# The carried row of a running prefix sum: an accumulating transfer sent by POOL in place of a plain transfer and a one-row addition on DVE

## The reference, cut to what matters

```
Tv = cheb(k)[:, :, :, j] * v                       # j = 0 .. 5 terms
kv_prefix = cumsum(Tv, over the 1024 positions)    # per batch row
ks_prefix = cumsum(cheb(k).sum(-1), over positions)
out = sum_j(Tq * beta * kv_prefix) / (sum_j(sum(Tq) * beta * ks_prefix) + 1e-7)
x = x + (out @ W_out.T) * silu(layernorm(moe(xn) + xn))
```

## Time and profile before

| | us |
|---|---|
| median of 3 runs | 885.68 |
| lowest, highest | 882.62, 885.87 |
| the profiled execution's own time | 883.1 |
| its span | 881.3 |
| DVE busy | 652.7 (74%), 1667 instructions |
| PE busy | 583.4 (66%) |
| ACT busy | 444.7 (50%) |
| POOL busy | 434.3 (49%) |

### The profile page before, as it was taken

How to read it: one execution, slowest core, us unless ns; L and a number is a source line. 1 busy time by engine, 2 the same in 40 slices (tenths; PEclk the granted TensorE clock), 3 DMA queues, 4 the chain that set the end, 5 groups by cost and what they waited for, 6 DMA issues and landing times.

```text
span 881.3 us, 21985 instructions
## 1 busy us (share of the span) xinstructions
PE 583.4 (66%) x7047; PEld 394.8 (45%) x7047; DVE 652.7 (74%) x1667; ACT 444.7 (50%) x1075; POOL 434.3 (49%) x697
## 2 busy tenths in 40 slices
PE   1888788878788878853544277777777777732120
PEld 0465555555555555542222145555555555421110
DVE  4588777777777777755878078989898989737766
ACT  1365555545555555521343277878787878400001
POOL 3134444544444555442777444444444444277873
PEclk9999999999999999985575599999999999955555
DMA  9920000000000000000111303333333332112221
GB/s 236 344 59 3 3 3 0 0 0 0 0 0 0 0 0 0 2 1 12 52 49 66 99 25 97 97 97 97 97 97 97 97 97 97 36 48 66 57 66 51
DMA packets 64527, 49.53 MB, mean 56 GB/s; under 512 B 10057, under 2 KB 55377, under 8 KB 64465
## 3 DMA queue, kind: packets, MB, share of 16 engines
q1 hardware_dynamic: 59328, 39.74, 14.4%
q0 software_dynamic: 5136, 9.02, 3.8%
HBM read 18.83 MB, written 18.35 MB: 42 GB/s over the span
## 4 chain that ended last, share of the span: by engine, by line
PE 32%; DVE 24%; POOL 17%; issue 17%; ACT 5%; DMA 2%; DVEq 2%; SPq 0%; POOLq 0%; ACTq 0%
POOL experts_sb L541 7%; POOL xbuf L528 7%; PE m_ps L988 4%; PE p_ps L869 4%; PE e_ps L1000 4%; DVE yts L1306 3%; PE q_ps L899 2%; PE y_ps L951 2%; ACT vd L603 2%; PE p_ps L944 2%; DVE x_all L1151 2%; DVE pr L1303 2%; DVE rot L1120 2%; ACT xs L608 1%; PE y_ps L832 1%
## 5 line engine op out<-in xcount | busy, mean ns | idle before, releaser
L576 ACT ACTIVATE pexp<-e_ps 128x512 f32<-128x512 f32 x128 | 76.4, 597 | 76.3 <-PE e_ps L816 74.7
L988 PE MATMUL m_ps<-xs,wb 128*128 128x512 f16 x276 | 80.6, 404 | 19.7 <-issue 18.4
L1087 DVE TENSOR_REDUCE mneg<-m_ps 128x4 bf16<-128x512 f32 x128 | 84.5, 681 | 5.1 <-PE m_ps L783 5.0
L541 POOL DMA_INDIRECT experts_sb<-ybuf,slots x64 | 66.1, 1033 | 28.7 <-issue 18.5
L528 POOL DMA_INDIRECT xbuf<-x,slots x64 | 63.3, 990 | 33.9 <-issue 19.2
L492 POOL COPY xs<-xs 128x128 f16<-128x128 f16 x32 | 12.8, 400 | 107.3 <-ACT xs L608 107.3
L603 ACT COPY vd<-p_ps 64x64 f32<-64x64 f32 x128 | 27.0, 211 | 73.1 <-DVE early L1122 70.8
L1046 PE MATMUL e_ps<-b_sb,cwt 8*128 8x128 f32 x64 | 16.6, 436 | 63.7 <-ACT cwt L744 63.7
L832 PE MATMUL y_ps<-pexp,vd 128*32 128x128 f32 x512 | 55.1, 284 | 2.7 <-ACT pexp L576 0.6
L1262 DVE TENSOR_SCALAR early<-p_ps 128x256 f32<-128x256 f32 x32 | 13.6, 424 | 55.3 <-ACT vs L650 55.3
L960 PE MATMUL p_ps<-eye_sb,yn 128*128 128x128 f32 x32 | 11.6, 364 | 63.7 <-DVE yn L1311 63.7
(11 more groups left out here) (218 smaller groups left out, 2125.6 us busy)
## 6 DMA issues: line engine op xcount, KB each, us to landing
wb<-experts_sb SPq DMA_DIRECT2D x46, 256.0 KB, 2.4
xbuf<-zero_sb SPq DMA_DIRECT2D x23, 256.0 KB, 4.3
xs<-xbuf SPq DMA_DIRECT2D x23, 256.0 KB, 3.0
ybuf<-rt SPq DMA_DIRECT2D x23, 256.0 KB, 2.5
experts_sb<-in_experts_w SPq DMA_DIRECT2D x8, 512.0 KB, 6.5
x_all<-in_x SPq DMA_DIRECT2D x8, 256.0 KB, 5.5
xbuf<-x,slots POOLq DMA_INDIRECT x64, 2.2
experts_sb<-ybuf,slots POOLq DMA_INDIRECT x64, 2.6
```

Of the source, the lines that this page charges most:

```text
L541: nc.gpsimd.indirect_dma_start(yg[:, 2 * (B * n + b) + k, :], None, ybuf, bass.IndirectOffsetOnAxis(ap=slots[:, k, B * n + b:B * n + b + 1 ...
L576: nc.scalar.activation(pexp[:, j, :, :], e_ps[j % 2][:, :, :], ACT.Exp, scale=float(D) ** -0.5).then_inc(exp_ready.sem, 1)
L988: last = nc.tensor.matmul(u_ps[f % 2], wb1[:, i % 2, f, a, :], xg16[:, i % 2, b, :], start=k == 0, stop=k == len(PARTS) - 1)
L1087: nc.vector.tensor_reduce(mneg[:, n.batch, j // 2, (j % 2) * NG:(j % 2) * NG + NG], m_ps[j % 2][:, :, :], AX.X, ALU.max, negate=True).then ...
```

## The change

The addition on DVE (L1286) and SP's plain transfer (L424) are taken out. In their place POOL sends one transfer per block, from row 127 of `last_sb` onto row 0 of `kv`, which adds to its destination. `last_sb` has four buffers where it had two; `carry` is gone. POOL sends it for blocks 4 to 7 between the scatters (after tiles 13, 17, 21 and 25), for blocks 8 to 30 inside the passes (before the third quarter of pass c-8), and for block 31 behind the last pass. POOL waits before it for the fifth step of that block's keys (L1283) and for ACT's copy. PE's `sums(c)` now waits for the transfer's semaphore.

```diff
--- before.py
+++ after.py
@@ -28,7 +28,7 @@
 SW = C + H
 E, FF = 8, 512
 FB = FF // P
-CHEB1, CHEB2 = 7, 8
+CHEB1, CHEB2 = 6, 8
 _ALPHA = np.arange(1, ORD + 2, dtype=np.float32) ** -1.5
 _BETA = np.cumsum(_ALPHA[::-1])[::-1][1:].astype(np.float32)
 BETA = [float(v) for v in _BETA / _BETA.sum()]
@@ -101,7 +101,7 @@
 
 def keys_steps(c):
 
-    return CHEB1 * c - min(c, B)
+    return CHEB1 * c
 
 
 def after(engine, sem, value):
@@ -236,8 +236,7 @@
         tb_ps = t_ps[:, :, :].rearrange("p a b -> p (a b)").bitcast(BF16)
 
 
-        carry = early[0:1, 0:B * ORD * SW].rearrange("p (b w) -> p b w", b=B)
-        last_sb = early[:, 0:2 * ORD * SW].rearrange("p (b w) -> p b w", b=2)
+        last_sb = early[:, 0:B * ORD * SW].rearrange("p (b w) -> p b w", b=B)
 
         y2, e2, res0, acc0 = (xs[:, i, :, :, :].rearrange("p h s d -> p (h s d)").bitcast(F32).rearrange("p (b c) -> p b c", b=B)
                               for i in range(4))
@@ -418,18 +417,11 @@
                 after(sp, s_rows_transposed, i - 1)
                 sp.dma_start(xin[:, i % 2, :, :], xbuf[SLOT * i:SLOT * i + SLOT, :].rearrange("(k p) c -> p k c", p=P)).then_inc(s_rows_in[i % 2], 16)
 
-            def carry_row(c):
-
-                sp.wait_ge(s_carry_copied, c + 1)
-                sp.dma_start(carry[0:1, c % B, :], last_sb[P - 1:P, c % 2, :]).then_inc(s_carry[c % B], 16)
-
             def store(i):
 
                 sp.wait_ge(s_y_copied, i + 1)
                 sp.dma_start(ybuf[SLOT * i:SLOT * i + SLOT, :].rearrange("(k p) c -> p k c", p=P), ysb[:, i % 2, :, :]).then_inc(s_rows_out[i % 2], 16)
 
-            for c in range(LEAD - 1):
-                carry_row(c)
             weights_split.wait(sp, Tile(TAUS - 1, 3))
             sp.wait_ge(s_owner, 1)
             for i in range(2):
@@ -446,8 +438,6 @@
                     load_up(i + 2)
                 if 0 < i <= PASSES:
                     store(i - 1)
-                if c < NT - B:
-                    carry_row(c)
                 if 0 <= i < PASSES - 2:
                     load_down(i + 2)
             for n in range(TAUS):
@@ -527,9 +517,17 @@
                 for k in range(2):
                     nc.gpsimd.indirect_dma_start(xbuf, bass.IndirectOffsetOnAxis(ap=slots[:, k, n:n + 1], axis=0), x16[:, n, :], None).then_inc(s_scattered, 16)
 
+            def add_carry(c):
+
+                pool.wait_ge(s_keys, keys_steps(c) + 5)
+                pool.wait_ge(s_carry_copied, c - B + 1)
+                pool.dma_start(kv[0:1, c % 2, :], last_sb[P - 1:P, c % B, :], accum_op=ALU.add).then_inc(s_carry[c % B], 16)
+
             def low_parts(i):
 
                 for f in range(FB):
+                    if f == 2:
+                        add_carry(i + LEAD)
                     pool.wait_ge(s_gelu, 2 * (FB * i + f) + 2)
                     after(pool, s_pass_done, i - 1)
                     nc.gpsimd.tensor_tensor(hid[i % 2][:, 1, f, :], gel[f], hid[i % 2][:, 0, f, :], ALU.subtract).then_inc(s_low, 1)
@@ -553,8 +551,12 @@
             pool.wait_ge(s_slots, 1)
             for n in range(NT):
                 scatter(n)
+                if n % 4 == 1 and 4 * 3 < n < 4 * 7:
+                    add_carry(n // 4 + 1)
             for i in range(PASSES):
                 low_parts(i)
+            for c in range(PASSES + LEAD, NT):
+                add_carry(c)
             pool.wait_ge(s_rows_out[0], 16 * ((PASSES + 1) // 2))
             pool.wait_ge(s_rows_out[1], 16 * (PASSES // 2))
             gather(0)
@@ -665,10 +667,9 @@
                 if not 0 <= c < NT - B:
                     return
                 act.wait_ge(s_outs, CHEB2 * c + 2)
-                if c >= 2:
-                    act.wait_ge(s_carry[(c - 2) % B], 16 * ((c - 2) // B + 1))
-                nc.scalar.copy(last_sb[96:P, c % 2, 0:3 * SW], cc_ps[0][96:P, 0:3 * SW])
-                nc.scalar.copy(last_sb[96:P, c % 2, 3 * SW:5 * SW], cc_ps[1][96:P, 0:2 * SW]).then_inc(s_carry_copied, 1)
+                after(act, s_carry[c % B], 16 * (c // B))
+                nc.scalar.copy(last_sb[96:P, c % B, 0:3 * SW], cc_ps[0][96:P, 0:3 * SW])
+                nc.scalar.copy(last_sb[96:P, c % B, 3 * SW:5 * SW], cc_ps[1][96:P, 0:2 * SW]).then_inc(s_carry_copied, 1)
 
             def oc_copy(c):
 
@@ -948,6 +949,7 @@
                 pe.wait_ge(s_keys, keys_steps(c + 1))
                 after(pe, s_outs, CHEB2 * (c - 1) + 2 if c else 0)
                 after(pe, s_carry_copied, min(c, NT - B))
+                after(pe, s_carry[c % B], 16 * (c // B))
                 nc.tensor.matmul(cc_ps[0][:, 0:3 * SW], tri_sb[:, :], kv[:, c % 2, 0:3 * SW], start=True, stop=True)
                 nc.tensor.matmul(cc_ps[1][:, 0:2 * SW], tri_sb[:, :], kv[:, c % 2, 3 * SW:5 * SW], start=True, stop=True).then_inc(s_summed, 1)
 
@@ -1280,10 +1282,7 @@
                 done(nc.vector.scalar_tensor_tensor(t[:, 4, :, 0:C], poly[:, 1, :, :], -0.078125 * C5, t[:, 0, :, 0:C], ALU.add, ALU.mult))
                 after(dve, s_summed, c - 1)
                 done(nc.vector.tensor_tensor(sums[:, :, 0:C], t[:, :, 1, 0:C], vs[:, c % 2, :].unsqueeze(1).to_broadcast([P, ORD, C]), ALU.mult), False)
-                done(nc.vector.tensor_reduce(sums[:, :, C:SW], t[:, :, 1, 0:C].rearrange("p j (h d) -> p j h d", d=D), AX.X, ALU.add), c >= B)
-                if c >= B:
-                    dve.wait_ge(s_carry[c % B], 16 * (c // B))
-                    done(nc.vector.tensor_tensor(kv[0:1, c % 2, :], kv[0:1, c % 2, :], carry[0:1, c % B, :], ALU.add), False)
+                done(nc.vector.tensor_reduce(sums[:, :, C:SW], t[:, :, 1, 0:C].rearrange("p j (h d) -> p j h d", d=D), AX.X, ALU.add), False)
                 done(nc.vector.tensor_reduce(t[:, :, 0, C:SW], t[:, :, 0, 0:C].rearrange("p j (h d) -> p j h d", d=D), AX.X, ALU.add), False)
                 assert at[0] == keys_steps(c + 1)
```

## The result

| | before | changed |
|---|---|---|
| median, us (11 runs each) | 884.07 | 887.59 |
| lowest, us | 882.23 | 886.49 |
| profiled execution, us | 883.1 | 890.24 |
| its span, us | 881.3 | 888.0 |
| DVE busy, us | 652.7 | 608.2 |

The ratio is 1.0041, 95% interval [1.0028, 1.0054]: 2.5 to 4.8 us slower, about 0.4%, which the forecast counted as "no change, on the slow side". One of the eleven changed runs took 941.33 us in a disturbed state and is left out of the ratio.

What follows compares the result with a forecast made beforehand. POOL's queue beside the scatters and ACT's path in the turns were taken as the bound; +3.2 us for four sends and -0.9 for the last addition gave +2.3, 888.0 us on the median, range 881.5 to 893.

Steps and rivals of the forecast that it cites:

- no change, on the slow side: Whole kernel: +2.3 us, under the about 0.5% (4.4 us) that a measurement can tell from no change.
- What bounds the kernel: Second stage: POOL's queue is the clock from 412 to 499 us, then ACT's path sets the 10.72 us turn.
- the 0.84 us in front of `up`: Steady turns: PE's idle time after DVE's transpose, read as the spare time of the DVE path.
- The busy shares: Steady turns, rival 1: DVE's time passes on; strong form 20 us faster, 868; 15% with weak form, a third of it strong.
- Four sends between the scatters: POOL's queue beside the scatters: four accumulating transfers at 0.8 us each, +3.2 us, bounds 2.2 and 5.0.
- rival 2: Between the scatters: POOL's accumulating transfer is dear, measurable loss from 1.33 us each; 895 at 2.5 us each; 20%.
- The addition in the last chain: Last turns: outputs follow DVE's keys directly, so removing the addition gains 0.9 us, bounds 0 and 1.8.
- SP's transfer: SP's queue, 28 transfers removed: later weight loads come earlier but nobody waits for them, 0 us.
- POOL didn't wait for DVE between the scatters: First new transfer: block 4's fifth step ends 0.5 us before POOL needs it; any wait bounded by some 0.5 us.
- the sends inside the passes: Before the third quarter: 0.56 to 1.26 us each fits POOL's 1.78 us of idle time, 0 us.
- PE's new wait: PE's `sums` in the passes: the row is sent 8.4 us before it is needed, 0 us.

Runs made afterwards that it cites:

- e6: Kernel of e1_split with one of ACT's four polynomial steps done by DVE: 865.60 us, ratio 0.9799 to the kernel before, 884 condition.
- e7: Kernel before with one of ACT's four polynomial steps done by DVE: 865.65 us, ratio 0.9799, 884 condition.
- e4: Kernel before with the row's addition done twice for each block, second result unused: 888.45 us against 883.13, ratio 1.0054.
- e9_plain: Kernel of e1_split plus four plain POOL sends of the row to a scratch row between the scatters: 892.32 us, ratio 0.976, 915 condition.
- 884 condition: Runs in which the kernel before takes 883 to 884 us, the result and second set of experiments; what makes the condition isn't known.
- e8: Changed kernel with three more POOL sends to HBM behind each accumulating one inside the passes: 886.45 us, ratio 1.0043 to the kernel before.
- e2_early: Changed kernel with only blocks 4 to 7 by accumulating transfers, 8 to 31 carried the old way: 892.90 us, ratio 0.977, 915 condition.
- e0_changed: Changed kernel run again without edit: 893.93 us, ratio 0.977 to the kernel before, 915 condition.
- e13: Kernel before with two of ACT's polynomial steps moved to DVE, output shifted by 3%: 907.75 us, ratio 0.991, 915 condition.
- e3: Changed kernel with the carry left out, neither transfer nor addition: 901.09 us, ratio 0.985 to the kernel before, 915 condition.
- 915 condition: Runs in which the kernel before takes 915 to 916 us, first and third set of experiments; what makes the condition isn't known.
- e1_split: Changed kernel with blocks 4 to 7 carried the old way, 8 to 31 by accumulating transfers: 903.91 us, ratio 0.988, 915 condition.

## Why the prediction was right

**What bounds the kernel: right.** POOL's queue beside the scatters, and the loop of ACT and PE in the turns. That DVE's addition lies on a path with idle time was shown three times: by the changed kernel (0.40 became 2.28, turn 10.72), by e6 against e7 (0.0 us), and by e4, where a second addition per turn costs 0.34 us. One reading under it was wrong: the 0.84 us in front of `up` are not what bounds DVE's path. In e4 0.62 of them were left while the turn had grown, since the clip is late for ACT's first polynomial step before the transpose is late for `up`. That ACT's work sets the turn was shown by e7: 0.39 us of it taken off, the turn 0.39 shorter. The busy shares, by which DVE was the bound, would have given 20 us.

**Four sends between the scatters: the mechanism right, the single send dearer.** Forecast 4 x 0.8 = 3.2 us, measured 3.91 for the four sends and 2.8 to 3.8 for the stretch, inside the bounds. The reason given for 0.8 was wrong: the transfer was put near the plain direct ones because it is direct. e9_plain's are at 0.54 to 0.59 us, where an accumulating one takes some 0.4 us more. It stays under the 1.33 from which rival 2 would decide. In the 884 condition the split alone was not run without another edit. That the sends are the loss there rests on the stretch of the scatters (in the changed kernel and again in e8), on the 3.5 us between the medians, and on e6 against e7.

**The addition in the last chain, -0.9 us: wrong.** This is the step that failed. The last keys did become shorter, but the outputs behind them also need PE's `sums`, and the chain of waits shows only the path that ended last. In the trace of before PE's had ended at 763.97 + 0.65 = 764.62 us. In the changed kernel DVE starts 0.10 us behind their end, so in before its outputs (764.96) would have started at 764.72 at the earliest: an estimate of 0.24 us for the missing addition, not 0.9. In the changed kernel `sums` took (1.75 + 1.04) - (0.94 + 0.65) = 1.2 us more at the lower clock, and DVE waits 2.30 us for them. With `sums` as slow as that, the addition is worth nothing. Two like pairs show it: e2_early, which still has it, waits 1.35 us for PE, and e0_changed 2.28, with 10.40 and 10.39 us from the last output step but two to the next; e7_before_poly waits 0.62 and e6_split_poly 1.52, with 9.80 and 9.76. e2_early:

```profile
770.07 0.90 DVE L1298 TENSOR_TENSOR kv<-kv,early 1x720 f32<-1x720 f32 x1
770.89 0.80 DVE L1299 TENSOR_REDUCE early<-early 128x80 f32<-128x640 f32 x1
773.05 0.60 DVE L1315 TENSOR_TENSOR pr<-early,y_ps 128x432 f32<-128x432 f32 x1 [1.35 <-PE q_ps L964]
```

What lowers the clock there isn't settled. It is low in every trace but those of before and of e4_twice (8.95 and 9.03 us at this place), in kernels that carry the last block in the new way, in the old way (e2, e7, e13) and not at all (e3), so the way of carrying it is not the cause. The bound of 0 that was given for this term was the right value. Without it the forecast's sum is +3.2 on the median of before.

**At nothing, and nothing:** SP's transfer, the sends inside the passes (0.77 us in 1.78; e8_four had room for three more), PE's new wait (the row lands after 1.9 us in the median, 2.8 at most, and is needed 8.4 us after sending). All this is for the 884 condition, and POOL didn't wait for DVE between the scatters there. In the 915 condition it did, by 7.80 us in e0_changed, where the forecast had bounded this by 0.5: the bound was drawn from DVE's turn of 9 us beside the scatters, which doesn't hold there. Nor does the 0 for SP's transfer: the forecast asked only whether a load ends PE's waits in the steady turns (rows 3), and not what stands behind the carried rows in SP's queue in front of pass 0.

**The total.** 888.0 was forecast and 887.59 measured. That they are 0.4 us apart is luck: the end was put 0.9 too good and the four sends up to 0.7 too low, while the median of three runs from which the forecast started, 885.68, was 1.6 above that of eleven. The difference was forecast as +2.3 and is +3.5. In the 915 condition the forecast would have been wrong, also as to sign: the change is 2.3% faster there.

**The better version.** e7_before_poly, which has nothing of the change, is 2.0% faster than the kernel before, and e6_split_poly is its equal. What was to be shortened is ACT's loop and not DVE's.

## What to carry to other kernels

An engine's busy share says nothing of what its instructions are worth. Look for the idle time in front of each link of its path within one period, and add the engine's work once more, or take some off its neighbour, to see which loop is the clock. A transfer taken off a compute engine is only free if its sender has idle time at that place: in the 884 condition the same send was free in 24 places and cost most of its duration in the four where the sender's queue was the chain. A transfer that nobody seems to wait for can still hold up what stands behind it in its queue: in the 915 condition SP's carried rows did that to the load on which the passes start. After moving work between engines look again at which instructions now lie beside each other: a move that shortened the loop by 0.39 us worked, and the next of the same size lost 0.20, since another engine's access fell on the last step of the path.

## What the runs showed of the hardware

- POOL sends an accumulating transfer of one row of 2.8 KB from SBUF to SBUF in 0.88 to 1.07 us between indirect ones and in 0.77 us between its subtractions. A plain one at the first place takes 0.54 to 0.59 us.
- In the 915 condition DVE instructions that wait for DVE's own predecessor stood some 1.1 us behind it while POOL sent indirect transfers and for some time after (in e1_split to 502.33 us, the last send is at 493.12), and SP's six sends for the weights took 23.6 us instead of 6.2. In e0_changed the last gap lies inside a break in the sending of 7.80 us, in e9_plain they ended with one of 3.13 us, while the 1.37 us before it didn't end them, and in e2_early they ended without one. The kernel before takes 32 us more in this condition. It wasn't traced there, but e13_before_two, which carries its rows in the same way, takes 50.19 us from the last scatter to the first output step beside the passes, where before takes 15.92 in the 884 condition: 34.3 us more. Whether the scatters' traffic or their sending holds the signals back, and what makes the condition, wasn't tried. The sign of the change differs between the two conditions.
- A DVE instruction beside POOL's subtraction doesn't get slower by a factor: 0.29 became 1.09 us, 0.90 became 1.83 and 0.29 became 1.17. Each is late by what was left of POOL's 1.15 us, less some 0.15: 0.95 were left and it was 0.80 late, 1.08 and 0.93, 1.02 and 0.88. The addition of e7, 1.32 us, fits as well (0.55 left, 0.42 late).
- With ACT's loop 0.39 us shorter, in e6 and in e7, two of the 22 turns are of the longer kind, in which PE is at the lower clock for a part, instead of seven. That was worth as much (5 x 1.65 = 8.3 us) as the shorter loop itself (22 x 0.39 = 8.6 us). Why it is so wasn't tried.
